# Adding each unit's results onto the normed tokens in DRAM, in place of two stored arrays of results

## The reference, cut to what matters

```python
out = X
for e in range(E):                                  # E = 8 experts, S = 2 of them for a token
    h = silu(einsum('btsd,dh->btsh', xs, W1[e])) * einsum('btsd,dh->btsh', xs, W3[e])
    y = einsum('btsh,hd->btsd', h, W2[e])
    out = out + where((topi == e)[..., None], y, 0.0).sum(axis=2)
...
xn = layernorm(x)
s = L0_attn_ref(xn, ...)
g = silu(L0_ffn_ref(xn, ...))
x = x + s * g
```

## Time and profile before

| | us |
|---|---|
| median of 3 runs (315.44 to 316.64) | 316.03 |
| the profiled execution | 315.75 |
| its span, first to last instruction | 314.0 |
| PE busy | 289.3 (92%) |
| DVE busy | 230.4 (73%) |
| ACT busy | 171.0 (54%) |
| POOL busy | 149.1 (47%) |
| TensorE clock granted, mean | 0.959 of full |

### The profile page before, as it was taken

The page is one execution under the profiler, slowest core; times in us unless marked ns, Lnnn a source line. Parts: engine busy times, 40 slices in busy tenths (PEclk is TensorE's granted clock), DMA queues, the critical chain, the costliest instruction groups (busy, mean ns, idle before and its releaser), DMA issues.

```text
span 314.0 us, 6542 instructions
## 1 busy us (share of the span) xinstructions
PE 289.3 (92%) x1973; PEld 255.7 (81%) x1973; DVE 230.4 (73%) x614; ACT 171.0 (54%) x361; POOL 149.1 (47%) x172
## 2 busy tenths in 40 slices
PE   8885795999999999999999998999999999997983
PEld 8774754899987989889998888999999999786331
DVE  3898887998598795768776785786776777574086
ACT  2889557576255975466646654455455554442031
POOL 2448878677114666376656742234344343334010
PEclk9955599999999999999999999999999999999998
DMA  6959714036210151112419649759786834940696
GB/s 188 348 174 324 224 49 145 29 90 181 70 33 20 42 153 51 36 43 69 109 52 154 181 126 352 247 194 319 263 287 243 312 99 151 335 133 13 226 382 195
DMA packets 42797, 52.17 MB, mean 166 GB/s; under 512 B 5622, under 2 KB 33530, under 8 KB 40844
## 3 DMA queue, kind: packets, MB, share of 16 engines
q1 hardware_dynamic: 36428, 40.57, 41.8%
q0 software_dynamic: 4320, 8.43, 8.1%
q10 hardware_dynamic: 2016, 2.76, 2.5%
HBM read 22.20 MB, written 14.26 MB: 116 GB/s over the span
## 4 chain that ended last, share of the span: by engine, by line
PE 65%; DVE 13%; issue 6%; ACT 6%; DMA 4%; POOL 2%; SPq 1%; POOLq 0%; DVEq 0%
PE bank L1485 12%; PE bank L1429 5%; PE bank L1438 5%; PE bank L1431 5%; PE bank L1430 5%; PE bank L1469 4%; PE bank L1440 4%; PE bank L1439 4%; PE bank L1486 4%; PE bank L1220 3%; PE bank L1221 3%; PE bank L1222 3%; PE bank L1531 3%; DMA early<-in_L_attn_x 3%; PE bank L1405 2%
## 5 line engine op out<-in xcount | busy, mean ns | idle before, releaser
L551 POOL DMA_INDIRECT y_dram<-stage,row x71 | 69.5, 978 | 104.4 <-DVE stage L1153 89.9
L542 POOL DMA_INDIRECT rows_dram<-rows,slot_row x64 | 68.4, 1068 | 25.3 <-issue 15.0
L735 ACT ACTIVATE stage<-bank 128x512 f32<-128x512 f32 x71 | 42.4, 598 | 69.4 <-PE bank L1431 40.2
L1485 PE MATMUL bank<-ew,hid_t 128*128 x284 | 73.0, 340 | 1.3 <-DVE stage L1153 0.7
L1485 PEld LDWEIGHTS bank<-ew,hid_t 128*128 128x128 f32 x284 | 53.4, 188 | 1.7 <-issue 1.6
L748 ACT ACTIVATE hid_t<-bank 128x512 fp32r<-128x512 f32 x71 | 40.8, 598 | 10.6 <-PE bank L1469 7.9
L1137 DVE TENSOR_TENSOR stage<-bank,stage 128x512 f32<-128x512 f32 x41 | 28.1, 686 | 17.5 <-PE bank L1431 17.0
L1429 PE MATMUL bank<-ew,row_t_hi 128*128 x82 | 34.6, 422 | 4.7 <-DVE row_t_lo L1131 4.5
L1486 PE MATMUL bank<-ew,hid_t 128*128 x164 | 36.4, 222 | 0.0
L1137 DVE TENSOR_TENSOR bank<-bank,stage 128x512 f32<-128x512 f32 x30 | 21.0, 699 | 17.8 <-PE bank L1440 17.7
L1431 PE MATMUL bank<-ew,row_t_hi 128*128 x82 | 32.3, 394 | 0.0
(11 more groups left out here) (178 smaller groups left out, 703.4 us busy)
## 6 DMA issues: line engine op xcount, KB each, us to landing
u<-ew SPq DMA_DIRECT2D x10, 1024.0 KB, 5.0
mix<-ew SPq DMA_DIRECT2D x5, 1024.0 KB, 5.5
stage<-in_L_ffn_W SPq DMA_DIRECT2D x15, 256.0 KB, 4.9
early<-in_L_attn_x SPq DMA_DIRECT2D x7, 512.0 KB, 4.8
row<-rows_dram SPq DMA_DIRECT2D x41, 64.5 KB, 2.0
xn_dram<-early SPq DMA_DIRECT2D x4, 512.0 KB, 4.0
u<-xn_dram SPq DMA_DIRECT2D x4, 512.0 KB
ew<-y_dram SPq DMA_DIRECT2D x8, 256.0 KB, 6.9
```

The costliest lines, as they stand in the source:

```text
L542: pool.indirect_dma_start(out=rows_dram[:, :], out_offset=bass.IndirectOffsetOnAxis(ap=slot_row[:, q % 2, at:at + 1], axis=0), in_=rows[:, ...
L551: pool.indirect_dma_start(out=y_dram[:, :], out_offset=bass.IndirectOffsetOnAxis(ap=row[:, k, D:ROW].bitcast(U32), axis=0), in_=y[:, t % Y ...
L735: act.activation(silu[:, t % 2], bank[:], ACT.Silu).then_inc(silu_done, 1)
L1485: pe.matmul(to, hi[:, at:at + P], w[c], start=(c == 0), stop=False, skip_group_check=True)
```

## The change

POOL's scatter of a unit's results becomes a scatter with addition (`compute_op=ALU.add`) onto `sum_dram`, an array with one row for each token and 256 more. The normed tokens are stored in its first 4096 rows, where `xn_dram` was. Each unit's rows name a token once, but different units meet on the same tokens, so the addition of step j waits until that of step j - 1 has landed, and at each phase's opening until the normed tokens' store has. Padding rows now have places behind the tokens in place of an index that is left out; they are zeros, made in the row buffer `rows` when its last use is over. At the end one array comes back.

```diff
-    y_dram = nc.dram_tensor("y_dram", (K * TOK, D), F32).ap()
-    xn_dram = nc.dram_tensor("xn_dram", (TOK, D), F32).ap()
+    sum_dram = nc.dram_tensor("sum_dram", (TOK + 2 * P, D), F32).ap()
...
+LAID_ON, LATER = (1, 2, 4, 5), 3
...
         rows = sb("rows", [P, ROWS, ROW], F32)
+        empty = rows[:, 0:2]
...
+        def place_of(c):
+            return tail_places[:, c % 4]
...
-            return banks[7] if j == FIRST_PAIR - 1 else turning(j)[1]
+            return banks[7] if j == FIRST_PAIR - 1 else banks[4] if j == J - 1 else turning(j)[1]
...
+        def load_sum(eng, c):
+            eng.dma_start(sum_all[:, c * CT:(c + 1) * CT, :], sum_tiles[:, c * CT:(c + 1) * CT, :]
+                          ).then_inc(sum_in[c], 16)
...
                 if g == LONE:
-                    sp.wait_ge(filled, 1)
-                    sp.wait_ge(made, 5)
-                    sp.dma_start(tiles_at(IDLE, 2), pad_rows).then_inc(pad_out, 16)
+                    sp.wait_ge(empty_made, 2)
+                    sp.dma_start(empty_tiles, empty[:, :, 0:D]).then_inc(empty_out, 16)
+                    sp.dma_start(tiles_at(IDLE, 2), empty).then_inc(pad_out, 16)
                     sp.wait_ge(planned, 2 * LONE + 3)
                     for start in loaded(mybir.EngineType.SP, 2 * J, E, IDLE - 2 * P):
-                        sp.dma_start(tiles_at(start, 2), pad_rows).then_inc(pad_out, 16)
+                        sp.dma_start(tiles_at(start, 2), empty).then_inc(pad_out, 16)
                     sp.wait_ge(pad_out, 16 * (E + 1))
                     stand(FIRST_PAIR)
...
-                    sp.wait_ge(c_ready, TILE[OPENS[LONE + 1]])
                 sp.dma_start(x_all[:, n, :], x_tiles[:, n, :]).then_inc(tail_in, 16)
-                sp.dma_start(xn_all[:, n, :], xn_tiles[:, n, :]).then_inc(tail_in, 16)
...
-            def scatter_result(j):
+            def empty_rows():
+                pool.wait_ge(sent[NG - 1][0], 16 * HALF)
+                pool.memset(empty[:, :, 0:D], 0.0).then_inc(empty_made, 1)
+                pool.iota(empty[:, :, D].bitcast(U32), [[P, 2]], base=TOK, channel_multiplier=1).then_inc(empty_made, 1)
+
+            def add_result(j):
                 pool.wait_ge(y_done, j + 1)
+                if j in OPENS:
+                    groups = -(-KNOWN[phase_of(j)] // GT) if phase_of(j) < LONE else NG
+                    for k in range(min(groups, 2)):
+                        pool.wait_ge(xn_out[k], (groups + 1 - k) // 2 * 16)
+                if j == FIRST_PAIR:
+                    pool.wait_ge(empty_out, 16)
+                if j:
+                    for t in range(TILE[j - 1], TILE[j]):
+                        pool.wait_ge(y_out[t % TURN], t // TURN * 16 + 16)
                 for t in range(TILE[j], TILE[j] + UNITS[j]):
                     k = t % TURN
                     pool.indirect_dma_start(
-                        out=y_dram[:, :],
+                        out=sum_dram[:, :],
                         out_offset=bass.IndirectOffsetOnAxis(ap=row[:, k, D:ROW].bitcast(U32), axis=0),
-                        in_=y[:, t % YB], in_offset=None,
-                        bounds_check=DUMP - 1, oob_is_err=False).then_inc(y_out[k], 16)
+                        in_=y[:, t % YB], in_offset=None, compute_op=ALU.add).then_inc(y_out[k], 16)
...
-            pool.memset(pad_row[:], 0.0).then_inc(filled, 1)
...
             for j in range(J + 1):
+                if j == FIRST_PAIR - 2:
+                    empty_rows()
...
-            for c in range(CHUNKS):
-                load_results(act, c, 1)
-            for c in range(CHUNKS):
-                act.wait_ge(sum_ready, c + 1)
-                act.activation(banks[c][:], banks[c][:], ACT.Silu).then_inc(silu2_done, 1)
+            for c in range(1, CHUNKS, 2):
+                load_sum(act, c)
+            for c in range(CHUNKS + LATER):
+                if c < CHUNKS:
+                    act.wait_ge(sum_in[c], 16)
+                    if c >= 4:
+                        place_left(act, c - 4)
+                    act.activation(place_of(c), chunk_of(sum_all, c), ACT.Silu).then_inc(silu2_done, 1)
+                if c - LATER in LAID_ON:
+                    act.wait_ge(res_ready, LAID_ON.index(c - LATER) + 1)
+                    act.activation(chunk_of(gated, c - LATER), banks[c - LATER][:], ACT.Copy).then_inc(res_copied, 1)
...
             for c in range(CHUNKS):
                 dve.wait_ge(silu2_done, c + 1)
-                dve.scalar_tensor_tensor(out=banks[c][:], in0=banks[c][:], scalar=0.5,
+                dve.scalar_tensor_tensor(out=place_of(c), in0=place_of(c), scalar=0.5,
                                          in1=chunk_of(gated, c), op0=ALU.mult, op1=ALU.mult).then_inc(prod_done, 1)
-                dve.wait_ge(prod_done, c + 1)
-                dve.tensor_tensor(chunk_of(gated, c), banks[c][:], chunk_of(x_all, c), ALU.add
-                                  ).then_inc(res_done, 1)
+                if c not in LAID_ON:
+                    dve.wait_ge(prod_done, c + 1)
+                    dve.tensor_tensor(chunk_of(gated, c), place_of(c), chunk_of(x_all, c), ALU.add
+                                      ).then_inc(res_done, 1)
...
-            for c in range(CHUNKS):
-                lay(chunk_of(xn_all, c), c, first=True)
+            for c in LAID_ON:
+                lay(chunk_of(x_all, c), c, first=True)
+            for c in LAID_ON:
+                pe.wait_ge(prod_done, c + 1)
+                lay(place_of(c), c, last=True).then_inc(res_ready, 1)
```

More of the change, by code:

```diff
@@ L37 @@
 EW = EC * P
-DUMP = K * TOK
 EPS = 1e-5
@@ L321, in chunk_of, with place_left @@
             return t[:, c * CT:(c + 1) * CT, :].rearrange("p i d -> p (i d)")
-        def sum_of(c):
-            return pair_sum[:, SUMS.index(c)]
+        def place_of(c):
+            return tail_places[:, c % 4]
+        def place_left(eng, c):
+            laid = sum(b <= c for b in LAID_ON)
+            if c in LAID_ON:
+                eng.wait_ge(res_ready, laid)
+            else:
+                eng.wait_ge(res_done, c + 1 - laid)
         flat = ew[:].rearrange("p c s d -> p (c s d)")
@@ L504, in _ @@
             for c in range(CHUNKS):
-                load_results(sp, c, 0)
+                if c % 2 == 0:
+                    load_sum(sp, c)
             for c in range(CHUNKS):
-                sp.wait_ge(res_done, c + 1)
+                copied = sum(b <= c for b in LAID_ON)
+                if c in LAID_ON:
+                    sp.wait_ge(res_copied, copied)
+                else:
+                    sp.wait_ge(res_done, c + 1 - copied)
                 sp.dma_start(out_tiles[:, c * CT:(c + 1) * CT, :], gated[:, c * CT:(c + 1) * CT, :]
@@ L530, in row_ids @@
                     half_sent(pool, q - 1, half)
-                pool.iota(rows[:, n:n + HALF, D].bitcast(U32), [[1, GT // 2], [TOK, K]], base=q * GT + n // K,
+                pool.iota(rows[:, n:n + HALF, D].bitcast(U32), [[1, GT // 2], [0, K]], base=q * GT + n // K,
                           channel_multiplier=NT).then_inc(ids_done, 1)
@@ L1058, in _ @@
             variance(1)
-            dve.wait_ge(made, 9)
+            dve.wait_ge(made, 8)
             for n in range(ROUTE_STEPS):
@@ L1383, in _ @@
             bias_of_h()
-            pe.wait_ge(made, 9)
+            pe.wait_ge(made, 8)
             places(0)
@@ L1463, in transpose_hidden @@
                 pe.wait_ge(hid_done, t + 1)
-                pe.wait_ge(hidt_lo_done, t)
+                pe.wait_ge(hidt_lo_done, t if j < J - 1 else t - 1)
                 if j == FIRST_PAIR - 1:
@@ L1533, in _ @@
             pe.wait_ge(y_done, J)
[L1534 to L1548 removed]
+            pe.wait_ge(tail_in, 16 * PARTS)
+            for c in LAID_ON:
[3 more added lines that the diff above has]
+                lay(place_of(c), c, last=True).then_inc(res_ready, 1)
 _INS = ["L0_attn_x", "L0_attn_W_re0", "L0_attn_b_re0", "L0_attn_W_im0", "L0_attn_b_im0", "L0_attn_W_re1",
```

59 lines of the change are left out of this document (13 added, 46 removed).

## The result

The changed kernel takes **384.51 us** (median of 6 runs, 382.48 to 390.43) against 315.99 us for the kernel before on the same chip: a ratio of 1.216, 95% interval 1.213 to 1.219. Forecast was 332, with a range up to 350. The direction was right and the size wrong, by 52 us. The profiled execution took 382.48 us with a span of 380.7, so the span grew by 66.7 us.

A forecast was written before the change was run, and what follows sets the result against it. PE, busy 92% of the span, was taken as the bound, then the chain of waits at the end. 315.75 + 13.3 padding + 2.3 clock + 7.1 chain - 6.8 tail = 331.65, forecast 332 us, range 320 to 350.

The forecast's parts named there:

- The padding, 13.3 us: At row 34, before the first pair: padding written late delays its row load, so PE stands still 13.3 us, bounds 8.6 to 16.5.
- the singles, put at nothing: Single tiles before the pairs: additions are further apart, with one or two row scatters between that cover the landing; no cost.
- the first additions, between 66 and 78 us: Early additions: each gets slower by about 0.4 us plus an addition's extra cost; POOL has idle time behind them, counted as nothing.
- The clock, 2.3 us: After PE's stall near row 34: 4.7 us at 1.2 in place of 2.4 GHz, worth 2.3 us, bounds 0 and 4.7.
- The chain, 7.1 us: Last two pairs and seven singles: each addition waits for the one before to land, making the end 7.1 us late.
- 0.77 + 1.27 + 2.2: A pair's step in the chain with a plain landing, 4.24 us, against the 4.85 us the chip needs for a pair.
- nine steps: Two pairs and seven singles at the chain's end, the only steps said not to fit with a plain landing.
- x: What an addition costs over a plain scatter: taken as 0.5 us, at least 0, at most about 2.0.
- my threshold of 0.6: Above an extra 0.6 us per addition, a pair's step passes 4.85 us and the whole row of 15 pairs counts.
- The tail, -6.8 us: The end: one 2 MB array returns in eight loads, not 4 MB in sixteen; 15.2 to 15.4 us against 22.2.
- The first, that additions are dear: Rival, chance 0.17: POOL's 0.97 us doubles per addition, a pair takes 6.18 us and a single 3.94; total 355 us.
- raised the chain by 4.6 us: Completion-order rule: additions beside weight loads land near 5 us; two pairs at 5.0 in place of 2.7, left out of the sum.

## Why the prediction was right or wrong

**The padding, 13.3 us: right as a mechanism and, by itself, nearly in size.** Alone it costs 17.6 us with its clock, against 15.6. In the changed kernel the stall is 25.9 us, 12.6 more, and each part can be read: POOL ends the addition of unit 29 at 194.87 where I had 185.14 (9.7); from there to the row load are 13.7 us where I had 11.0 (2.7); and the load took 4.5, not 4.3 (0.2). The 2.7 are mostly the landing of the padding: I took 2.5 us, with 4.3 as the bound, and the eight stores land 4.6 us after their issue in the median and 5.3 at most. The longer fill, 0.91 us in place of 0.20, costs nothing, because it runs beside the addition: SP's first store goes out 0.44 us behind the addition, where I had 0.46.

**The step that failed first: the singles, put at nothing.** The prediction gave a price to "the first additions, between 66 and 78 us" alone and said of the rest that their row scatters "cover the landing". A single's step on POOL has one addition and one or two row scatters: 1.57 + 0.30 and 1.28 for each scatter make 4.4 with two. And the landings are not covered: between 80 and 190 us, 12 of the 26 additions waited for one, 21.8 us together. POOL's last row scatter began at 191.03, where before it was at 181.54. It takes both: with additions but no waits it began at 185.13, with waits but plain scatters at 184.80 (181.74 in the changed kernel with plain scatters). With the padding early PE still waited 16.1 us, with plain scatters and the padding late 15.0. Two causes, POOL's lateness and the padding, lie beside each other at the same row load, and taking the one away uncovers the other. That, and the early stores' own collision with the chain, is why the early padding gave back 8.8 us and not 17.6.

**The clock, 2.3 us: right.** 4.9 us of work at half speed is worth 2.4. (By its own rows the prediction's stretch, 34 to 38.8, is 4.8 us and not 4.7, which is worth 2.4 too.)

**The chain, 7.1 us: the step that failed by most.** Three numbers were off in "0.77 + 1.27 + 2.2". The landing: I took 2.2, from the quiet stretch of the earlier trace rows, though the same rows had 3.2 and up to 6.0 beside the loads of weights. I put that inside a bound for single steps, as if a late landing were chance. It is not: with waits, the copy is released by the landing that the scatter follows, and nearly every step of a pair meets one, and the last ones the tail's loads. The chain alone shows it: 31.8 us with nothing dear in it, and on one chip a chain with small copies costs a third of one with whole copies, 7.9 us against 24.1. I charged nine steps with it; all 15 pairs and 7 singles pay, the pairs 2.0 us each over their pace of 4.85. Second, x was 0.5 and is about 1.1 (3.3 us against 2.2 where it is quiet; single steps 4.08 against 3.03 with plain scatters), beyond my threshold of 0.6 for the whole row of pairs. Third, POOL's instruction of 0.97 became 1.56, twice in a pair. The threshold was the right question, and my own formula at x = 1.2 already gave 312.5 (312.8, worked out again) for the chain's end without the padding; the value x = 0.5 was chosen by "the two reads can run side by side", which no row bore out. The prediction's own signs of being wrong named this case: POOL's instruction is no longer near 0.97 us, and the quiet landing is over 3.

**The tail, -6.8 us: right in sign, 2.9 too good.** The end has 18.4 us, where I had 15.3. The first product starts 4.4 us behind the first load (I had 3.8), DVE takes 9.8 us (8.7) with waits of 0.8 and 1.0 us for ACT, whose copies stand in order before its silus, and the last store ends 4.2 us behind DVE (2.7). PE's additions for these chunks ran at half clock, PE having been idle for 32.8 us before them: 1016 ns each in this group of the tail, and the clock of its windows there is 0.50.

```profile
L1546 PE MATMUL bank<-stage,ident 128*128 128x512 f32 x8 | 6.7, 1016 | 32.8 <-DVE stage L1223 32.8
...
369.00:372.00 3.00, 3.00 (x4) 1.33 (x5) 2.27 (x4) 1.69 (x3) 0.00 (x0) 0.50 0.54 183
```

**The rivals.** The first, that additions are dear, came nearest, at 355 us with 0.17, and its mechanism is half of what happened: it too has no copy beside the chain, which alone makes 31.8 us. It took the doubled instruction (1.94, measured 1.56) and 6.18 us for a pair (6.86) and 3.94 for a single (4.08). Against the profiled execution it is 27 us low: 12.6 by the longer stall, 9 by 13 steps of 6.86 in place of 6.18, 3 by the tail, and most of the rest on the way from row 34 to the first pair's addition, which waited 4.25 us for a landing at 233.49. In the sum of factors, chain alone +31.8, padding alone +17.6, both with the new tail and plain scatters +35.6, and the additions' price on top of those +32.9. These do not add up, since they overlap: chain, padding and new tail one by one would make 45.5 us and the three make 35.6 together. No single one of them is "the cause": the 71 additions cost about 6 us where nothing waits for them and 32.9 us in the chain.

**The packets, and the two rules that I had cited.** Of the changed kernel's queue that carries the scatters, and then of the one before, the page's packets, MB and share:

```profile
q0 software_dynamic: 12272, 8.89, 16.2%
...
q0 software_dynamic: 4320, 8.43, 8.1%
```

The 4320 are 32 for each of the 135 scatters, and the 12272 are 64 x 32 + 71 x 144: an addition of 128 rows makes 144 packets where a plain scatter makes 32. The runs bear this out, with 4320 packets for every kernel with plain scatters and 12272 for every one with additions, chain or none. The Trainium skill (Collectives: The Full Stack, The bandwidth ceiling) says of a reducing transfer that it emits two read descriptors where a copy emits one, and runs at half the rate. The trace agrees in direction; the factors here are 1.6 for the instruction, 1.5 for the quiet landing and 4.5 in packets, none of them 2. I had given this rival 0.17 because the trace of before had nothing on it; the rule was the only evidence there was. The other rule of the Trainium skill (DMA: Bandwidth & Descriptors, Queues, rings and completion order) is that a completion is counted only after earlier writes of the same DMA engine. By it I had raised the chain by 4.6 us and left that out of the sum. The landings of 3.9 us beside copies, and of 2.1 without, agree with it: the copy issued at 215.88 would land at about 220.6 by the medians of 4.6 and 4.8 us for copies there; the scatter issued behind it landed at 220.88. No run here separates this from a plain sharing of the DMA engines. But I applied it to two pairs, where the waits made it hold for nearly all fifteen.

## What to carry to other kernels

A wait for a landing puts the DMA's whole latency into the step, so it is to be costed with the latency beside whatever that same landing releases, whichever engine it releases, never with the quiet one. When two delays feed one wait, take their maximum, and expect that mending one gives back only what it has above the other. An operation whose price no row shows should be bounded by the rule that speaks of it, and if a threshold lies inside the bound, the case beyond the threshold deserves as much chance as the one before it.

## What the runs showed that was not expected

- An indirect scatter with addition, 128 rows of 512 bytes in float32, takes 1.56 us of POOL and lands 3.3 us after its start; the plain one 0.97 and 2.2.
- It makes 144 packets in place of 32.
- The same kernel took 316 us on some chips and 341 to 344 on others, with single executions from 315.4 to 317.8 on the first kind and from 338 to 346 on the second. Additions without a chain gain 3.5 to 4.7% on the two slower ones and lose 0.4% on the one of the others where they ran. The cause is open.
- The 128 x 256 fill of the padding took 0.91 us, beginning while POOL's addition was still being issued. In the runs with the late padding and plain scatters the same fill began as the scatter ended and took 0.33 and 0.35, and the 128 x 129 one 0.20. So its size is worth 0.15 us at most, and the addition beside it the rest.
